# Two-layer graph attention over 8192 nodes: moving the marks of begun rows to ScalarE and the diagonal of rows without edges to POOL

## What is computed

```
h  = relu(layernorm(x))
Wh = h @ W + b
e[i,j] = leaky_relu(Wh[i] . a1 + Wh[j] . a2, 0.2)
att = softmax over j of (e[i,j] where adj[i,j] > 0, else -9e15)
x  = x + att @ Wh
```

## Time and profile before

| what | value |
|---|---|
| median of 3 runs | 1870.39 us (1869.71 to 1871.53) |
| the profiled execution's own time | 1869.14 us |
| its span in the profile | 1867.4 us |
| mean granted TensorE clock | 0.655 |
| DVE busy | 1103.5 us (59%) |
| PE busy | 943.0 us (50%) |
| POOL busy | 804.9 us (43%) |
| ACT busy | 551.3 us (30%) |
| DMA | 344.52 MB, 184 GB/s in the mean |

### The profile page before, as it was taken

One profiled execution on the slowest core, in us unless ns is written; L12 is line 12 of the kernel. 1 busy time (PEld: TensorE's weight loads), 2 busy tenths in 40 slices (PEclk: granted clock), 3 DMA queues, 4 the chain that ended last, 5 costly groups with the idle time before them and its releaser, 6 DMA issues.

```text
span 1867.4 us, 23293 instructions
## 1 busy us (share of the span) xinstructions
PE 943.0 (50%) x6148; PEld 655.9 (35%) x6148; DVE 1103.5 (59%) x5065; ACT 551.3 (30%) x790; POOL 804.9 (43%) x1095
## 2 busy tenths in 40 slices
PE   2544473544545355455647656666232244454554
PEld 1322252322323233333334333443232234444444
DVE  2666566887887868778786765767221132333343
ACT  3433463333333333353343454553000000000000
POOL 3433453232333153344344433323555656666664
PEclk8766776666667766767766677776555566555555
DMA  8656697554564675576767788882221222333332
GB/s 347 214 203 219 227 338 262 209 206 164 212 229 156 219 259 209 208 273 215 258 253 265 268 298 282 314 320 69 50 42 39 49 52 60 62 68 63 70 72 58
DMA packets 105142, 344.52 MB, mean 184 GB/s; under 512 B 20241, under 2 KB 77841, under 8 KB 88625
## 3 DMA queue, kind: packets, MB, share of 16 engines
q1 hardware_dynamic: 39712, 277.76, 38.7%
q0 software_dynamic: 21568, 44.90, 12.0%
q10 hardware_dynamic: 43728, 20.33, 4.0%
HBM read 326.01 MB, written 16.91 MB: 184 GB/s over the span
## 4 chain that ended last, share of the span: by engine, by line
DVE 26%; issue 25%; POOL 14%; DMA 14%; PE 13%; another core or an unknown queue 6%; ACT 1%; DVEq 1%; SPq 0%; ACTq 0%; POOLq 0%
POOL work L447 12%; DMA work<-node_table,source 7%; PE acc L571 6%; DMA x_old<-in_x_dram 4%; DVE row_list L842 3%; DMA node_table<-ext 3%; DVE slots L832 3%; PE packed L503 2%; PE ps_h L587 2%; DVE found L842 2%; DVE column L846 2%; DVE weights L1013 2%; DVE member L940 1%; DVE slots_b L846 1%
## 5 line engine op out<-in xcount | busy, mean ns | idle before, releaser
L447 POOL DMA_INDIRECT work<-node_table,source x674 | 650.5, 965 | 327.7 <-issue 197.2
L659 ACT ACTIVATE work<-adj_sb 128x2048 fp8e4<-128x2048 int32 x256 | 485.9, 1901 | 35.5 <-DMA adj_sb<-in_adj_dram 12.7
L571 PE MATMUL acc<-work,weights 128*128 128x129 f32 x1348 | 296.2, 389 | 290.4 <-DVE weights L1013 183.3
L571 PEld LDWEIGHTS acc<-work,weights 128*128 128x128 f32 x1348 | 268.0, 294 | 310.6 <-issue 305.7
L503 PE MATMUL packed<-work,ident_h 128*128 128x512 fp8e4 x1024 | 348.2, 477 | 0.7 <-issue 0.7
L685 ACT ACTIVATE prob<-leaky 128x3 f32<-128x3 f32 (+4 forms) x148 | 28.4, 205 | 1059.6 <-DVE leaky L984 900.7
L423 POOL TENSOR_TENSOR rstd<-var_eps,minus_half 128x1 f32<-128x1 f32 x128 | 77.5, 608 | 526.3 <-DVE var_eps L775 526.3
L973 DVE TENSOR_TENSOR z<-ps_s,work 128x3 f32<-128x3 f32 (+4 forms) x148 | 23.4, 163 | 457.7 <-remote 259.1
L1013 DVE TENSOR_SCALAR weights<-row_name,row_of,prob 128x128 f32<-128x128 f32 x674 | 189.7, 357 | 33.9 <-PE acc L571 33.0
L503 PEld LDWEIGHTS packed<-work,ident_h 128*128 128x128 f16 x1024 | 124.3, 126 | 130.1 <-issue 81.1
L522 PE MATMUL ps_list<-list_hi,member 128*128 128x19 bf16 (+3 forms) x337 | 28.8, 186 | 223.5 <-DVE member L940 198.0
(11 more groups left out here) (134 smaller groups left out, 1332.1 us busy)
## 6 DMA issues: line engine op xcount, KB each, us to landing
adj_sb<-in_adj_dram SPq DMA_DIRECT2D x128, 2048.0 KB
work<-node_table,source POOLq DMA_INDIRECT x674
node_table<-ext ACTq DMA_DIRECT2D x128, 65.0 KB
x_old<-in_x_dram ACTq DMA_DIRECT2D x64, 64.0 KB
x_after_layer<-x_new ACTq DMA_DIRECT2D x64, 64.0 KB
x_old<-x_after_layer SPq DMA_DIRECT2D x64, 64.0 KB
out_dram<-x_new SPq DMA_DIRECT2D x64, 64.0 KB
x_in<-in_x_dram ACTq DMA_DIRECT2D x13, 256.0 KB, 5.5
```

The lines of the kernel that those rows point to most:

```text
L447: pool.indirect_dma_start(out=gathered[:, g % LIST_SLOTS, c, :], out_offset=None, in_=table[l], in_offset=bass.IndirectOffsetOnAxis(ap=sou ...
L571: pe.matmul(to, weights[:, w % WEIGHT_SLOTS, :], gathered[:, g % LIST_SLOTS, c, 0:DIM + 1], start=(not u.last and e is u.lists[0] and c == ...
L659: nc.scalar.activation(sign[:, k % 2, QCOLS * q:QCOLS * (q + 1)], adj_sb[:, n % ADJ_SLOTS, QCOLS * part:QCOLS * (part + 1)], ACT.Relu, sat ...
```

## The change

It does four things.

1. For the 60 lists with one part, ScalarE makes `begun` in place of DVE. The triangular matrix for the first places holds -0.125 in place of 1, so that what PE gives is minus an eighth of the offset; `relu(0.125 * (place + 1) - 0.125 * offset)` is above zero from the row's first place on. `count_h` counts from 1, and the lines that use it are adapted (`word_part`, `rank`, and `member`, where the multiplication becomes a logical and). Lists with two or eight parts still mark on DVE.
2. So that ScalarE has the offsets early, DVE's copy of them (`keep_offsets`) moves from the tail of the round to its head: behind `leak` and ahead of `finish`, in rounds 1 to 6 behind `choose_pending` and ahead of `find_edges`.
3. ScalarE's marking (`begin`) stands between `exp` and `cast_ahead(k, 1)`, in rounds 0 to 6 at the end of the round, behind the last cast.
4. POOL makes the diagonal `lone` of the same 60 tiles in layer 0, at the head of its round, with a semaphore of its own for PE. Layer 1's stay on DVE.

```
+            def mark_lone(l, u):                      (POOL)
+                if not pools_lone(l, u):
+                    return
+                n, e = finish_index(l, u.tile), u.lists[0]
+                pool.wait_ge(degree_known, e.order + 1)
+                if n >= 2:
+                    pool.wait_ge(x_done, n - 1)
+                pool.tensor_scalar(lone[:, n % 2, :], ident[:], degree[:, e.id:e.id + 1], None, ALU.is_gt).then_inc(lone_pooled, 1)
...
+                for u in SUMS.get(k, []):
+                    mark_lone(0, u)
                 for t in tiles_of(SUMS.get(k - 2, [])):
                     node_sums(1, t)
...
+            def begin(e):                             (ACT)
+                p, n = e.order % 2, e.chunks * TILE
+                act.wait_ge(offset_kept, e.order + 1)
+                if e.order >= 2:
+                    act.wait_ge(member_ready, e.order - 1)
+                nc.scalar.activation(begun[:, p, 0:n], count_h[:, 0:n], ACT.Relu, bias=row_list[:, p, 0:1], scale=0.125, saturate=False) \
+                    .then_inc(begun_ready, 1)
...
                         cast_ahead(k, q)
+                    for e in EXTRACT.get(k, []):
+                        if e.parts == 1:
+                            begin(e)
                     continue
...
                     exp(0, e)
+                for e in EXTRACT.get(k, [])[:1]:
+                    if e.parts == 1:
+                        begin(e)
                 cast_ahead(k, 1)
...
             def keep_offsets(e):                      (DVE)
                 p = e.order % 2
                 dve.wait_ge(offset_ready, e.order + 1)
-                return step(nc.vector.tensor_copy(row_list[:, p, 0:2], ps_list[:, 0:2]))
...
+                nc.vector.tensor_copy(row_list[:, p, 0:2], ps_list[:, 0:2]).then_inc(offset_kept, 1)
...
-                kept = keep_offsets(e)
-                dve.wait_ge(dve_steps, kept)
+                dve.wait_ge(offset_kept, e.order + 1)
+                settle()
                 high = step(nc.vector.tensor_copy(list_hi[:, p, OFF_C:OFF_C + width], row_list[:, p, 0:width]))
-                begin = step(nc.vector.tensor_scalar(begun[:, p, 0:n], count_h[:, 0:n], row_list[:, p, 0:1], None, ALU.is_ge, saturate=False))
...
-                dve.wait_ge(dve_steps, begin)
+                if e.parts > 1:
+                    dve.wait_ge(dve_steps, begin)
+                else:
+                    dve.wait_ge(begun_ready, BEGUN_OF[e.id] + 1)
...
                 choose_pending()
+                if e.parts == 1:
+                    keep_offsets(e)
                 find_edges(e)
...
                 for e in lists_of(units):
                     leak(0, e)
+                for e in head:
+                    if e.parts == 1:
+                        keep_offsets(e)
                 for u in done:
                     finish(0, u)
```

More of the change, by code:

```diff
@@ L151 @@
             GATHERED[_l][_e.id] = _slots[G_OF[_l][_e.id] % LIST_SLOTS]
+BEGUN_OF = {}
+for _e in sorted(LISTS, key=lambda e: e.order):
+    if _e.parts == 1:
+        BEGUN_OF[_e.id] = len(BEGUN_OF)
 IN_ORDER = [[e for u in us for e in u.lists] for us in SUM_ORDER]
@@ L319, in x_of, with pools_lone, lone_index @@
             return x_in[:, (m // X_GROUP) % X_SLOTS, m % X_GROUP, :] if m < TILES else x_new[:, (m - TILES) % 4, :]
+        def pools_lone(l, u):
+            return l == 0 and len(OF_TILE[u.tile]) == 1
+        def lone_index(l, u):
+            mine = pools_lone(l, u)
+            return sum(pools_lone(0, v) == mine for v in SUM_ORDER[0][:U_OF[0][id(u)]] if v.last) if l == 0 else \
+                sum(not pools_lone(0, v) for v in SUM_ORDER[0] if v.last) + sum(v.last for v in UNITS[:U_OF[1][id(u)]])
         def load_x_old(eng, l, t):
@@ L383, in _ @@
             pool.memset(ident[:], 0.0).then_inc(constants, 1)
-            pool.memset(before[:], 1.0).then_inc(constants, 1)
+            pool.memset(before[:, 0, :], -0.125).then_inc(constants, 1)
+            pool.memset(before[:, 1, :], 1.0).then_inc(constants, 1)
             pool.memset(mean_row[:, DIM:DIM + 1], 1.0).then_inc(constants, 1)
             pool.memset(list_lo[:, :, ROW_C:ROW_C + 1], 0.0).then_inc(constants, 1)
-            pool.wait_ge(constants, 6)
+            pool.wait_ge(constants, 7)
             pool.affine_select(out=ident[:], in_=ident[:], compare_op=ALU.not_equal, fill=1.0, base=0,
@@ L474, in _ @@
             pe.wait_ge(weights_loaded, 7 * 16)
-            pe.wait_ge(constants, 7)
+            pe.wait_ge(constants, 8)
             for l in range(LAYERS):
@@ L561, in sum_unit @@
                 if u.last:
[L562 removed]
+                    pe.wait_ge(lone_pooled if pools_lone(l, u) else lone_done, lone_index(l, u) + 1)
                     pe.wait_ge(mean_kept, l + 1)
@@ L795, in _ @@
             dve.wait_ge(weights_loaded, 7 * 16)
-            dve.wait_ge(constants, 7)
+            dve.wait_ge(constants, 8)
             for l in range(LAYERS):
@@ L951, in choose_sources @@
                 dve.wait_ge(list_turned, e.order + 1)
-                step(nc.vector.tensor_tensor(rank[:, p, 0:c], place[:, 0:c], lists[:, :, OFF_C:OFF_C + 1].rearrange("p c o -> p (c o)"),
-                                             ALU.subtract))
+                step(nc.vector.scalar_tensor_tensor(out=rank[:, p, 0:c], in0=lists[:, :, OFF_C:OFF_C + 1].rearrange("p c o -> p (c o)"),
+                                                    scalar=8.0, in1=place[:, 0:c], op0=ALU.mult, op1=ALU.add))
                 step(nc.vector.tensor_copy(row_of[:, e.base:e.base + c], lists[:, :, ROW_C:ROW_C + 1].rearrange("p c o -> p (c o)")))
@@ L987, in mark_lone @@
             def mark_lone(l, u):
-                if not u.last:
+                if not u.last or pools_lone(l, u):
                     return
```

22 lines of the change are left out of this document (14 added, 8 removed).

## The result

The changed kernel takes 1928.9 us, the median of 4 runs (1921.04 to 1933.13), against 1870.05 us before (4 runs, 1866.61 to 1871.53). The ratio is 1.0313, with an interval of 1.0271 to 1.0354: slower by 58.9 us. The direction was forecast, the size was not: the time lies 28 us above the 1901 us and 11 us above the range. The profiled execution took 1932.62 us, with a span of 1930.9 us.

What follows compares the result with a forecast made beforehand. DVE was taken to bound the lists up to 1040 us. Lists 43.4 - 17.3 = +26.1, plus 6.0 and 3.0, is +35; less 3, from 1869.1 us, gives 1901 us, range 1870 to 1918.

Steps and rivals of the forecast that it cites:

- The new wait: At the list rounds' heads, DVE's early copy waits for PE's offsets: 43.4 us; rounds 1 to 5 lose 6.0 us.
- the DMA-heavy stretch: Lists from 1040 to 1245 us, DMA at 0.84: waits in rounds 47 to 60 may be covered, 3 us off.
- What costs nothing: ACT's marking, which holds back `cast`, and POOL's `lone`, which fits into its wait for `var_eps`, were priced at nothing.
- The 3.0 us forecast for it: Round 6: ACT's marking delays the last `store_table` by 3.05 us, and all gathers wait for it; 3.0 us taken.
- What the tail saves: DVE's list-round tails without `lone`, copy and `begun`: 31.5 us saved, 17.3 counting where scores do not wait for gathers.
- The sum: Whole kernel: 26.1 us for the list stage + 6.0 + 3.0 = +35 us, 3 taken off, giving 1901 us.
- The offsets in time: Rival: PE's offsets are ready at the heads, so the copy hardly waits; 1851 to 1866, say 1861 us; chance 0.12.
- quick heads: Rival: PE runs all heads as in round 44, 21 us of waits in place of 44; about 1881 us; chance 0.15.
- no change: Rival: DVE's waits for `slots` and gathers shrink by what the head takes; 1870 us; chance 0.09.
- The heavier one: Rival: the saved tail is lost everywhere to gathers or late `x_old` loads; 17 us more, 1918 us; chance 0.10.
- The signs promised: In the profile after: copy waits 35 to 60 us, DVE's busy time falls 40 to 50, ACT's rises about 40.

Runs made afterwards that it cites:

- The copy alone: The change with marks and diagonals back on DVE, so only the offsets' copy moves to the head: 1924.79 us, ratio 1.0291.
- idle copies: Kernel before plus five unneeded ACT copies per round with a one-part head list: ahead of the second cast 1898.72 us, behind it 1860.64 us.
- both repairs: The change with PE's offsets ahead of the first quarter of `pack` and ACT's marks behind the second cast: 1872.67 us, ratio 0.9983.
- the mark behind the cast: The change with ACT marking behind its second cast, in round 6 behind the last table store; copy still early: 1909.46 us, ratio 1.0208.
- the late load in the list rounds: Kernel before, the matrix tile's first-half load waiting for the third cast instead of the second, from the tenth tile on: 1909.98 us, ratio 1.0201.
- midway: The change with DVE's copy between `edge_keys` and `edge_tops`, and ACT's marks behind the second cast: 1856.99 us, ratio 0.9907.
- the late first half: Kernel before, the load of each matrix tile's first half waiting for the third cast instead of the second, in all rounds: 1877.25 us, ratio 1.0085.

## Why the prediction was wrong in size

- **The new wait** (43.4 us in the lists, 6.0 in rounds 1 to 5, less 3 for the DMA-heavy stretch, so 46.4): right. The copy alone cost 50.4 us, with 52.2 us of waits in the heads of one part; in the change, where the scores wait longer first, it was 39.2. (One reading behind it was not quite right: before the change one of these copies, round 28's, did wait 1.8 us. The sum does not use it.)
- **What costs nothing: the step that failed.** The text said that ACT's marking "also holds back `cast` by the wait and itself, but ACT is busy 320 of 831 us". A busy share says that the casts get done, not that they are done in time. The one that stands behind `begin` releases a load of the matrix, and the load's moment decides when the gathered rows land. Priced at nothing, ahead of the cast in place of behind it, it cost 1928.9 - 1909.46 = 19.4 us as the times stand, 21.4 against the kernels before of each chip. This is the difference between two places, and the second may be better than no work at all: idle copies cost 25.7 us ahead of the cast and gained 12.4 behind it. Against marks left on DVE, ACT's marks ahead of the cast cost 13.8 us net of all that they save. A part of the 21.4 may be the last table store in round 6, which the same edit brought back ahead of the mark. The 3.0 us forecast for it are not shown: by the timelines round 8's scores start at 236.8 us with the change, and at 240.7 and 236.3 in the two runs with the early copy and no mark on ACT.
- **What the tail saves** (17.3 us that count): roughly right. With the copy early and nothing held back, moving marks and diagonals off DVE gave 50.4 - 37.5 = 13.0 us, which may hold some of the gain of work behind the cast. The rule of the Trainium skill (VectorE: DVE Perf Modes, "The DRAIN you can't avoid"), by which an estimated 28.6 us would have counted, has an exception in the same paragraph, which the prediction left out: a next instruction that is not held starts earlier. Round 30 agrees with the exception: the diagonal and the mark taken out last 0.76 us, and 0.40 was saved.
- **The sum.** Measured, term by term: 50.4 - 13.0 + 21.4 = 58.8 us. (Each is a difference of neighbouring kernels, so that they add up says nothing; that both repairs together give the time of before, and that idle copies ahead of the cast cost 25.7 us, does. What work behind the cast gains would make the tail and the held cast smaller by the same amount.) Forecast in the same order: 46.4 - 17.3 + 3.0 = 32.1. Of the 27 us missing, 18 are the held cast, 4 the wait and 4 the tail.
- **The rivals.** The offsets in time, quick heads and no change fell with the copies' 47.6 us. The heavier one came nearest in time, 1918, by a mechanism that the runs do not bear out: with the cast not held back 13.0 us of the tail's saving were there, and the wait for `x_old` grew by 5.0 us only. Its neighbour, gathers that come later than before, was in no case; I took their delay as given, so the range ended too low.
- **The signs promised.** Copies waiting in 30 to 40 heads, 35 to 60 us: 33 heads of one part, 39.2 us. ACT's busy time up by about 40: up by 40.5. DVE's down by 40 to 50: down by 21.1. There I counted the full durations of instructions that overlap others, which I had not done for the tail: the 60 diagonals, 0.28 us each, took 7.7 us off in the run that moves them alone, and 1.7 in the change, not 17. Rounds 1 to 6 later by 7 to 10 us: 11.3, which proves little, since kernels whose node rounds are those of before end them between 207.5 and 214.9 us. The second layer as long as before: from the last `ext` of the first, 539 us against 545, and 532 to 549 in the other runs. ACT's mark of 384 columns took 0.61 us in the mean, where about 0.45 was estimated. POOL's diagonal: 0.66 us, between the bounds of 0.28 and three times that, and hidden in its wait for `x_new`.

PE's granted clock in the list stage fell from 0.69 to 0.66. It is 0.68 with the mark behind the cast, where PE also waits less; what of the change's loss the clock makes was not separated; the late load in the list rounds lost its 39.7 us at 0.69.

## What to carry to other kernels

Before an instruction that waits is put into an engine's queue, ask what each instruction behind it releases, transfers above all; a low busy share answers another question. A value is best fetched where it is surely ready and not yet needed: the same copy cost 50 us ahead of `x_new`, while at the tail and midway its one-part heads wait 2.0 and 3.4 us in all. And where a sum takes a wait for DMA as given, one case should move it.

## What the runs showed of the hardware

- The scores' wait for gathers depends on when another queue's load is issued: 70.8 us before, 115.2 with ACT's second cast 1.3 us late (mean of the list rounds), 125.8 with the load some 4 us late.
- Five copies of 0.28 us that nobody needs, put behind the second cast, made the kernel 12 us faster (ratio 0.9898). They put off the third and fourth cast and the later issues of ACT's queue; which of these gains was not tried.
- In rounds 1 to 6 the late first half gains where in the list rounds it loses: 25.9 us earlier to the end of the nodes. Up to there the mean granted clock was 0.81 in place of 0.75 and the DMA engines' share 0.73 in place of 0.69; what causes what was not tried.
- POOL takes 0.66 us in the mean for the diagonal of 128x128 floats that takes DVE 0.28 us.
